# Three of sixteen expert splits done two stages earlier, kept in DRAM and read back whole

## The reference

```python
x = x + _L0_xattn_ref(_layernorm(x), ctx_512, ...)   # 16 heads, 1024 context rows in each of 16 batches
x = x + _L0_attn_ref(_layernorm(x), w_qkv, w_o)      # 32 query and 4 key heads of 64, 64 tokens a batch
...
x = hidden_states.reshape(-1, H)                     # 1024 tokens of 512
w, sel = _route(x, gate_weight, expert_bias)         # 4 of 16 experts for each token
def body(acc, inp):
    g, u, d, we = inp
    y = jax.nn.silu(x @ g.T) * (x @ u.T) @ d.T       # 512 -> 256 -> 512
    return (acc + we[:, None] * y, None)
shared = jax.nn.silu(x @ shared_gate.T) * (x @ shared_up.T) @ shared_down.T
return (out + shared).reshape(B, S, H)
```

## Time and profile before

| what | us |
|---|---|
| median of 3 runs (1441.41 to 1449.11) | 1446.62 |
| profiled execution, its own time | 1441.12 |
| its span, first to last instruction | 1439.3 |
| PE busy | 1342.3 |
| POOL busy | 549.5 |
| DVE busy | 792.5 |
| ACT busy | 728.0 |

### The profile page before, as it was taken

The page is one execution under the profiler, slowest core; times in us unless marked ns, Lnnn a source line. Parts: engine busy times, 40 slices in busy tenths (PEclk is TensorE's granted clock), DMA queues, the critical chain, the costliest instruction groups (busy, mean ns, idle before and its releaser), DMA issues. The chain is left out here.

```text
span 1439.3 us, 22817 instructions
## 1 busy us (share of the span) xinstructions
PE 1342.3 (93%) x7136; PEld 1102.6 (77%) x7136; DVE 792.5 (55%) x1388; ACT 728.0 (51%) x1736; POOL 549.5 (38%) x337
## 2 busy tenths in 40 slices
PE   7999899999999999999987999998899989999991
PEld 6777678888887878787866888887788768787771
DVE  5444565756666666666555454445388833433245
ACT  3444565656556565656545777777221223333330
POOL 4421414142323233241103333334034395238975
PEclk9998999999999999999998999999899999999996
DMA  6886350413223241413042334432642166546767
GB/s 241 271 289 194 134 185 21 181 53 140 93 95 124 67 166 46 187 44 117 1 175 76 103 111 140 138 110 96 237 183 102 75 229 202 185 134 213 253 190 227
DMA packets 79128, 209.66 MB, mean 146 GB/s; under 512 B 5904, under 2 KB 39184, under 8 KB 73104
## 3 DMA queue, kind: packets, MB, share of 16 engines
q1 hardware_dynamic: 69616, 163.65, 32.9%
q0 software_dynamic: 7136, 38.80, 8.1%
q10 hardware_dynamic: 2304, 6.29, 1.1%
HBM read 154.46 MB, written 92.01 MB: 171 GB/s over the span
## 5 line engine op out<-in xcount | busy, mean ns | idle before, releaser
L809 DVE TENSOR_TENSOR probsT_lo<-psTr,probsT_hi 128x512 fp32r<-128x512 f32 x256 | 176.6, 690 | 166.0 <-ACT probsT_hi L762 165.6
L762 ACT CAST probsT_hi<-psTr 128x512 fp32r<-128x512 f32 x256 | 149.9, 586 | 197.8 <-PE psTr L896 194.0
L896 PE MATMUL psTr<-ident,probs 128*128 128x128 f32 x1024 | 153.6, 274 | 11.9 <-DVE probsT_lo L809 5.9
L896 PEld LDWEIGHTS psTr<-ident,probs 128*128 128x128 f32 x1024 | 124.2, 141 | 51.3 <-DVE probsT_lo L809 14.5
L804 DVE TENSOR_REDUCE nmax<-psS 128x1 f32<-128x1024 f32 x128 | 155.4, 1214 | 7.7 <-PE psS L81 6.7
L717 ACT ACTIVATE probs<-psS,nmax 128x1024 f32<-128x1024 f32 x128 | 143.6, 1122 | 8.8 <-DVE nmax L804 8.8
L673 POOL TENSOR_TENSOR w_slots<-ctx_f,w_slots 128x512 fp32r<-128x512 f32 x32 | 41.3, 1292 | 279.2 <-ACT w_slots L724 279.2
L79 PE MATMUL psV<-probsT_hi,w_slots 128*128 128x512 f32 x256 | 114.9, 449 | 0.7
L79 PE MATMUL psS<-w_slots 128*128 128x512 f32 x256 | 112.6, 440 | 2.7 <-DVEq L797 2.0
L79 PE MATMUL bank<-w_slots,ao_first_hi 128*128 (+1 forms) x244 | 103.8, 425 | 5.9 <-issue 2.9
L1640 POOL TENSOR_TENSOR w_slots<-w_ahead,w_slots 128x3072 fp32r<-128x3072 f32 x15 | 102.2, 6811 | 1.2
(11 more groups left out here) (300 smaller groups left out, 3266.2 us busy)
## 6 DMA issues: line engine op xcount, KB each, us to landing
w_ahead<-w_exp POOLq DMA_DIRECT2D x14, 1536.0 KB, 7.4
qe<-stage SPq DMA_DIRECT2D x16, 1024.0 KB, 6.9
w_slots<-qe SPq DMA_DIRECT2D x15, 1024.0 KB, 5.1
wraw<-w_pairs SPq DMA_DIRECT2D x7, 1792.0 KB, 11.8
early<-xs SPq DMA_DIRECT2D x47, 256.0 KB, 2.7
xs<-h_rows SPq DMA_DIRECT2D x47, 256.0 KB
early<-ctx SPq DMA_DIRECT2D x16, 512.0 KB, 9.8
ao<-attn_out SPq DMA_DIRECT2D x32, 256.0 KB, 2.9
```

The source lines that it names most:

```text
L762: act.copy(PT[k % PTN].hi[:], psT[slot][:]).then_inc(turned_hi, 1)
L809: dve.tensor_tensor(out, psT[slot][:], f32(hi), ALU.subtract).then_inc(turned_free, 1)
L896: last = pe.transpose(psT[slot][:, q * P:(q + 1) * P], src(q), ident[:])
```

## The change

The experts 7, 10 and 13 are no longer split by POOL in the expert stage. Their raw weights are read in three pieces of 128x1024 each in the self stage, split there by POOL (`pre_high`, `pre_low`) and written to a new DRAM tensor `w_pre` by SP (`pre_moves`). In the expert stage `whole_load` brings high and low part into the slot with two transfers of 1.5 MB, and `whole_ready` counts `w_ready` up when they have landed. POOL takes the experts in the order `TAKEN` = 1 to 5, 7, 6, 8, 10, 9, 11, 13, 12, 14, 15, and tells them ready in `ORDER` = 0 to 6, 8, 7, 9, 11, 10, 12, 14, 13, 15; the table's numbers (`READY`) follow.

Because the self stage now uses `w_ahead`, the output projection's raw parts are loaded in its last eight steps. The transfers that fill `xs` with zeros, 18 as before, now all stand in cross attention: three in each of the rounds 1 to 6. The semaphores of cross attention are cleared and used again, and three small tiles of the expert stage lie in `gate_f`.

```diff
...
+FILLS = 3
...
+            if not (first or last):
+                fill(FILLS * i - FILLS)
             if not last:
-                fill(2 * i)
                 for j in range(2):
                     load_kv(2 * i + 2 + j)
...
-            if not last:
-                fill(2 * i + 1)
+                if not (first or last):
+                    fill(FILLS * i - FILLS + 1 + j)
...
-WO_STEPS = (2, 4, 6, 7)
+WO_STEPS = (0, 1, 2, 3)
+PIECES, PIECE = 3, KC * BANK // 2
+PRE_FIRST, PRE_STEP, NPRE = 7, 3, NT // 2 - 1
...
-            if g == 2 and not last and not isinstance(i, int):
-                r = 2 * NT - 4 + 2 * i + v // HKV
-                sp.dma_start(t["xs_r"][r], t["zeros"]).then_inc(keep["fill_in"], 16)
+
+        def pre_moves(i, v, last):
+            g = v % HKV
+            if g < PIECES and has_before(i, v):
+                m = i - 1
+                sp.wait_ge(pre_lo, PIECES * m + g + 1)
+                for part, src in enumerate((p_high[g], p_raw[g])):
+                    sp.dma_start(t["w_pre"][m, part, g], src).then_inc(p_out[g], 16)
+            if g >= 1 and has_group(v, last):
+                m = i
+                if isinstance(i, int):
+                    if v == HKV + 1:
+                        sp.wait_ge(w_ready, WCH)
+                else:
+                    sp.wait_ge(p_out[g - 1], 32 * m)
+                sp.dma_start(p_raw[g - 1], t["w_exp"][PRE_STEP * m + PRE_FIRST + 1, :, (g - 1) * PIECE:g * PIECE]).then_inc(
+                    p_in[g - 1], 16)
...
+            if g == 3 and has_group(v, last):
+                pre_low(i, 0)
+            if g < 2 and has_before(i, v):
+                pre_low(i - 1, g + 1)
             if ahead(1):
                 norm(u + 1, (v + 1) % 2)
+            if g >= 2 and has_group(v, last):
+                pre_high(i, g - 2)
+            if g == 0 and has_before(i, v):
+                pre_high(i - 1, 2)
...
+        def pre_high(m, j):
+            pool.wait_ge(p_in[j], 16 * m + 16)
+            pool.sem_inc(pre_seen, 1)
+            pool.tensor_copy(p_high[j].bitcast(F32R), p_raw[j]).then_inc(pre_hi, 1)
+
+        def pre_low(m, j):
+            pool.wait_ge(pre_hi, PIECES * m + j + 1)
+            pool.tensor_tensor(p_raw[j].bitcast(F32R), p_raw[j], p_high[j], ALU.subtract).then_inc(pre_lo, 1)
...
+WHOLE = tuple(PRE_FIRST + PRE_STEP * m for m in range(NPRE))
+SPLIT = tuple(e for e in range(1, NE) if e not in WHOLE)
+ORDER = sorted(range(NE), key=lambda e: e + 1.5 * (e in WHOLE))
+TAKEN = sorted(range(1, NE), key=lambda e: e - 1.5 * (e in WHOLE))
+READY = [max(ORDER.index(a) for a in range(e + 1)) for e in range(NE)]
...
+        def whole_load(e):
+            for part in range(2):
+                pool.dma_start(f32(slot(e)[part]).rearrange("p (s c) -> p s c", s=PIECES),
+                               t["w_pre"][WHOLE.index(e), part].rearrange("s p c -> p s c")).then_inc(whole_in, 16)
+
+        def whole_ready(e):
+            pool.wait_ge(w_ready, ORDER.index(e))
+            pool.wait_ge(whole_in, 32 * (WHOLE.index(e) + 1))
+            pool.sem_inc(w_ready, 1)
...
-            pool.tensor_copy(slot(e)[0], raw[(e + 1) % 2]).then_inc(pool_hi, 1)
-            pool.wait_ge(pool_hi, e)
-            expert_low(e)
-            if e + 2 < NE:
-                expert_load(e + 2)
+            if e in WHOLE:
+                whole_load(e)
+                continue
+            pool.tensor_copy(slot(e)[0], raw[j % 2]).then_inc(pool_hi, 1)
+            pool.wait_ge(pool_hi, j + 1)
+            expert_low(e, j)
+            if e - 1 in WHOLE:
+                whole_ready(e - 1)
+            if j + 2 < len(SPLIT):
+                expert_load(j + 2)
```

More of the change, by code:

```diff
@@ L1001, in build_self @@
     tab = sb("rope_s_tab", [P, 2, 3, DH // 2])
-    wo_raw = keep["ahead"] + [sb("wo_last", [P, KC, BANK])[:]]
+    wo_raw = [sb("wo_first", [P, KC, BANK])[:]] + keep["ahead"]
+    sets = [a.rearrange("p k x -> p (k x)") for a in keep["ahead"]]
+    p_raw, p_high = ([a[:, j * PIECE:(j + 1) * PIECE] for a in sets] for j in range(2))
+    p_in, p_out = keep["pre_in"], keep["pre_out"]
+    pre_seen, pre_hi, pre_lo = sem("pre_seen"), sem("pre_hi"), sem("pre_lo")
     WO = [Shared(ws, c * WSZ, (KC, D)) for c in range(HQ // 2 // KC)]
@@ L1059, in plan, with has_group, has_before @@
         return GI * i + v, 2 * i + v // HKV, v % HKV, ahead
+    def has_group(v, last):
+        return not last and v >= HKV
+    def has_before(i, v):
+        return v < HKV and not (isinstance(i, int) and i == 0)
     def turns(eng, step):
@@ L1077, in _ @@
         sp.dma_start(raw[4], t["w_qkv"][4]).then_inc(w_in[4], 16)
+        for done in keep["cleared_later"]:
+            sp.sem_clear(done)
         def step(i, v, last):
             u, tt, g, ahead = plan(i, v, last)
[L1080 to L1083, removed]
+            pre_moves(i, v, last)
+            if last and v in WO_STEPS:
+                c = WO_STEPS.index(v)
+                if c:
+                    sp.wait_ge(p_out[c - 1], 32 * NPRE)
                 sp.dma_start(wo_raw[c], t["w_o"][:, c * KC:(c + 1) * KC, :]).then_inc(wo_in[c], 16)
@@ L1429 @@
 ON_WAY = 3
+WHOLE = tuple(PRE_FIRST + PRE_STEP * m for m in range(NPRE))
[3 more added lines that the diff above has]
+READY = [max(ORDER.index(a) for a in range(e + 1)) for e in range(NE)]
+assert WHOLE[-1] < NE - 1 and PIECES * PIECE == 2 * KC * I + NIT * D
 C_BIAS, C_TRI, C_TRIG, C_DIAG = 0, NE, NE + NE * NE, NE + NE * NE + NG * NG
@@ L1491, in build_moe @@
     cw = sb("choice_weight", [P, NT, TOPK])
-    full, cum, tabx = sb("tiles_of", [P, NE]), sb("tiles_to", [P, NE]), sb("table_cols", [P, 4])
+    full, cum, spare = (gate_f[:, j, :] for j in range(3))
+    tabx = sb("table_cols", [P, 4])
     pairs = cmp_e[:].rearrange("p i a j -> p (i a j)")[:, 0:NG * GS * GS].rearrange(
@@ L1637, in slot, with expert_low, expert_load @@
             return WS[:, at:at + wcol], WS[:, at + wcol:at + 2 * wcol]
[L1639 to L1644, removed]
+        def expert_low(e, j):
+            pool.tensor_tensor(slot(e)[1], raw[j % 2], f32(slot(e)[0]), ALU.subtract).then_inc(w_ready, 1)
+        def expert_load(j):
+            pool.wait_ge(w_ready, ORDER.index(SPLIT[j - 2]) + 1 if j >= 2 else 1)
+            pool.dma_start(raw[j % 2], t["w_exp"][SPLIT[j] + 1]).then_inc(pool_in[j % 2], 16)
+        def whole_load(e):
[6 more added lines that the diff above has]
+            pool.sem_inc(w_ready, 1)
         pool.sem_inc(a_lo, 1)
@@ L1657, in _ @@
         pool.sem_inc(w_ready, 1)
-        expert_load(2)
-        for e in range(1, NE):
+        expert_load(1)
+        for e in TAKEN:
             if e == NSLOT:
                 pool.wait_ge(table_made, 2)
[L1662 to L1665, removed]
+            if e in SPLIT:
+                j = SPLIT.index(e)
+                if j == 0:
+                    pool.wait_ge(raw_in[0], 32)
+                else:
+                    pool.wait_ge(pool_in[j % 2], 16 * ((j + 1) // 2))
+            if e == WHOLE[0]:
+                for j in range(PIECES):
+                    pool.wait_ge(keep["pre_out"][j], 32 * NPRE)
             if e == 1:
@@ L2213, in build @@
             build_self(nc, ctx, sem, t, keep)
+        second_sems.close()
         with ExitStack() as ctx:
```

33 lines of the change are left out of this document (19 added, 14 removed).

## The result

| | median us | before, same chips | ratio, 95% interval |
|---|---|---|---|
| the changed kernel, 11 runs | 1437.60 | 1446.51 | 0.9943 [0.9928, 0.9958] |
| once more in a later series, 12 runs | 1438.52 | 1446.10 | 0.9964 [0.9944, 0.9984] |

The change makes the kernel faster: 8.2 us in the first comparison (0.0057 of 1446.5) and 5.2 us in the second, 6.7 as their mean. The forecast was 6.5 us less and 1440.1 us. The first comparison lies just past half a per cent, the second just inside. The ratios leave out two executions at a far lower granted clock, one of the kernel before (1528.41 us at 0.833) and one of the kernel with POOL late (1697.46 us at 0.734); all others lie near 0.97.

A forecast was written before the change was run, and what follows sets the result against it. Up to 1309 us PE bounds the kernel, then POOL, whose gathers stand behind expert 15's split. Gathers 7.0 us earlier less 0.5 for DMA gave -6.5 us: 1440.1 us, 8-in-10 range 1433 to 1450.

The forecast's parts named there:

- POOL done 10.5 us earlier: Expert stage: with three splits taken out, POOL is through with expert 15 at 1371.0, 10.5 us earlier than before.
- Tile 38's landing as the gate: Start of the gathers: tile 38's store landing releases the first gather at 1375.9 instead of 1382.93, 7.0 us earlier.
- PE's wait for expert 12: Tile 36: expert 12's split ends at 1349.7, so PE's wait shrinks from 2.38 to about 1.4 us, a gain of 1.0.
- Issue of a pair: POOL's two whole loads of an expert: 0.56 us each, 1.1 a pair; upper bound 3.4 a pair.
- Self stage 0: Self stage: nine casts and nine subtractions fit into POOL's idle times, the subtraction taking 2.27 to 2.40 us; cost 0.
- One slip without effect: Cross attention's zero fills: two rounds lose two fills each and six get a third, at cost 0.
- The gathers' stretch unchanged: End of the kernel: the 32 gathers and their additions still take 52.9 us.
- Rival 3: Gathers: the earlier start also shortens their stretch, gain up to POOL's full 10.5 us, 1436 to 1439; chance 0.14.
- DMA in the expert stage: Whole loads, up to 14.8 us a pair, slow SP's row loads: 0.5 us for all three.
- rival 1: Expert stage: row loads starve behind whole pairs, PE waits 4.4 us three times, 13.2 us; 1452.8; chance 0.14.
- no wait of PE for `early<-xs` behind the stage's start: Sign in the profile after: PE waits for rows only twice, at the expert stage's start.

The follow-up runs named there:

- POOL late: The changed kernel with three more casts of expert 15's raw weights ahead of its split: 1441.86 us, 0.9967 to the kernel before.
- none whole: The changed kernel with its self stage work kept, but all fifteen experts split in the expert stage: 1445.22 us, 0.9995 to the kernel before.
- the kernel before with the overlap: The kernel before, with SP reading store landings up to four stores behind until tile 34: 1446.98 us, 1.0000 to the kernel before.
- the kernel that issued them in turn: The changed kernel with POOL taking experts in number order, whole loads behind the split in front: 1443.64 us, 0.9994 to the kernel before.
- with 2 KB: The changed kernel with split weights in DRAM as 2 KB rows: 1442.44 us, 0.9973; with SP's landings also read four stores behind: 1436.15 us, 0.9940.
- The fastest kernel: The changed kernel with SP reading each landing before the fourth store behind it up to tile 34: 1433.67 us, 0.9913 to the kernel before.
- its sister: The changed kernel with SP's landings read four stores behind and split weights in DRAM as 2 KB rows: 1436.15 us, 0.9940 to the kernel before.
- two of three experts: The changed kernel with one expert split in the expert stage again: 7 and 10 whole 1439.16 us, 0.9952; 10 and 13 whole 1440.52 us, 0.9971.
- The kernel with 12 KB: The changed kernel with split weights in DRAM as 128 rows of 12 KB for each part: 1444.49 us, 0.9992 to the kernel before.

## Why the prediction was right, and where it was off

**POOL done 10.5 us earlier.** Right. From tile 21 it was through at 101.7 us before and at 91.1 after, 10.6 us less.

**Tile 38's landing as the gate, 7.0 us for the first gather.** Right in mechanism and size: counted from tile 21, 7.6 us in the first profile and 8.5 in the second, with tile 38's landing as the release in both. The store was issued at 1375.62 and POOL began at 1378.55, 2.9 us later, where I had 2.25 + 1.0.

**PE's wait for expert 12, 2.38 to 1.4 us.** 0.7 us in one execution, 2.1 in the other. Where it is short, it is because a wait for rows at tile 35 came first (1.32 us), so the two are not to be added up.

**Issue of a pair, 1.1 us.** 1.5 us: 0.757 each in the mean. That lies between the bounds of 1.1 and 3.4, near the lower one, and makes expert 12 only 0.4 us later than I had it. At 384 pieces an extra cost shows, 0.2 us an issue, so the low end did not hold.

**Self stage 0.** Right. The subtraction took 2.39 us, within the bounds, and it went where it was said to go. POOL's timeline of one:

```profile
858.87 1.29 POOL L1158 TENSOR_TENSOR q_rope<-q_terms 128x512 f32<-128x512 f32 x1 [2.19 <-DVE q_terms L1291]
860.12 2.38 POOL L1202 TENSOR_TENSOR w_ahead<-w_ahead 128x1024 fp32r<-128x1024 f32 x1
863.03 1.04 POOL L1162 TENSOR_TENSOR sprobs<-sprobs,srinv 128x512 f32<-128x512 f32 x1 [0.53 <-DVE srinv L1313]
```

Of the 2.9 us of idling 0.53 are left, and the multiplication is still released by VectorE. By the kernel with none whole the earlier stages cost nothing, and by the upper end of its interval at most 1.0 us (1446.4 times 0.0007). One slip without effect: a single round of cross attention lost its two fills, not two rounds (14 fills and two less, six more, make 18).

**The gathers' stretch unchanged.** Right as far as single executions tell: from first gather to end 56.4 us before and 56.9 after, but 60.2 in the second profile of the changed kernel; 59.1 in the kernel before with the overlap, 54.9 to 59.7 in the others. Rival 3, a faster stretch, does not show.

**DMA in the expert stage, 0.5 us.** This is the term that failed. The bound for a pair, 14.8 us, was twice the landing of one load; the halves landed after 8.6 to 15.7 us, and a pair took up to 17.6 us in the kernel that issued them in turn. Against rival 1 I had argued that the row loads share and stand well ahead. They do share. But I had looked at one load and not at what it stands behind: SP reads the landing of a store first, I quoted that very line for the gate, and did not ask what it does when several stores in a row take longer than a tile. One of the signs named for the forecast failed, no wait of PE for `early<-xs` behind the stage's start: these waits were 3.1, 0 and 10.4 us in three executions of what is up to 1365 us the same program. Taking the habit away brought 5.8 us with 4 KB (0.9913 against 0.9943 and 0.9964, on other chips) and 4.8 us with 2 KB (0.9940 against 0.9973, on one chip), each uncertain by some 4. So rival 1 did occur, in part and by another way, at a price of about 5 us instead of 0.5. That the edit gains is shown by these times and by the kernel before, where it gains nothing; that it gains by the waits for rows is argued from the profiles of the kernels without it.

**Why the sum came out near.** The gain without that price is some 12 us (6.7 and 5) rather than 7, and the two misses cancel. That is luck: the gate and its 7 us were right, the closeness of the sum was not earned. The fastest kernel is 12.6 us under the one before. Of this the profiles show 5 to 9 (its 154.9 and the 152.7 of its sister, against 159.5 and 162.0); where the rest is, single executions that differ by 5 us among themselves don't show. It stays open.

## What to carry to other kernels

When a change makes transfers larger, look at every queue that reads a landing before its next issue. One landing longer than a round is made good by the next, as in the kernel before; several in a row make the queue fall behind, and what stands behind it comes late in turn. Reading landings a few rounds late, as deep as the buffers allow, gained about 5 us here and cost nothing in the kernel before. Once the next gate is reached (here tile 38's landing), moving more work away can't bring the gathers forward: with two of three experts the time could not be told from that with three. And a sum can come out right from two misses; only runs that take each part away tell.

## What the runs showed of the hardware

- Transfers of 1.5 MB from DRAM, one at a time, landed in 7.4 us in the median, two issued together in 8.6 to 15.7 us. Beside the pairs 256 KB stores took 4.7 us in the median and up to 8.4, where the fastest took 2.0.
- Larger pieces made the same transfer faster beside others with 2 KB pieces: with 12 KB the whole loads landed in 10.9 us in the median, with 4 KB in 11.3 to 12.7 (five executions with all three pairs), with 2 KB in 13.4 and 13.9. What that did to the row stores is not clear of noise (5.5; 4.4 to 5.8; 4.2 and 6.5 us). The kernel with 12 KB was 4 us slower than with 4 KB beside it by the ratios, 6 by the medians.
- POOL's issue of one transfer took 0.54 us for 128 pieces of 12 KB, 0.757 for 384 of 4 KB and 0.85 for 768 of 2 KB: more pieces cost, but far less than in proportion.
- The zero fills, now three a round in cross attention, landed in 17.1 us in the median instead of 10.6, and nobody waited for them.
